# A state-space scan in one ring of buffers, its step sizes summed on TensorE, and a mixer without square root

## The reference

```python
def _ssm_layer(x, A_log, Dp, W_dbc, W_dt, b_dt):
    A = -jnp.exp(A_log)
    dbc = jnp.einsum('ble,ce->blc', x, W_dbc)
    delta, Bm, Cm = jnp.split(dbc, [DT_RANK, DT_RANK + N_STATE], axis=-1)
    delta = jax.nn.softplus(jnp.einsum('blr,er->ble', delta, W_dt) + b_dt)
    dA = jnp.exp(delta[..., None] * A)
    dBx = (delta * x)[..., None] * Bm[:, :, None, :]
    ...
    _, hs = jax.lax.associative_scan(combine, (dA, dBx), axis=1)   # h = dA * h + dBx
    y = jnp.einsum('blen,bln->ble', hs, Cm)
    return y + Dp * x
```

## Time and profile before

| | |
|---|---|
| median of 3 runs | 6798.75 us (6796.87 to 6824.71) |
| the profiled execution | 6804.28 us, its span 6802.5 us |
| busy: PE, DVE, ACT, POOL | 72%, 93%, 72%, 89% |
| stage one | to about 6192 us |
| stage two | from there to the end |
| DMA | 1561 MB, mean 229 GB/s |

### The profile page before, as it was taken

How to read it: one execution, slowest core, us unless ns; L and a number is a source line. 1 busy time by engine, 2 the same in 40 slices (tenths; PEclk the granted TensorE clock), 3 DMA queues, 4 the chain that set the end, 5 groups by cost and what they waited for, 6 DMA issues and landing times. The chain is left out here.

```text
span 6802.5 us, 114118 instructions
## 1 busy us (share of the span) xinstructions
PE 4903.7 (72%) x32336; PEld 1829.8 (27%) x32336; DVE 6322.3 (93%) x4435; ACT 4927.0 (72%) x10217; POOL 6080.2 (89%) x1940
## 2 busy tenths in 40 slices
PE   5777777777777777777777777677777777774777
PEld 1222222222222222222222222222222222222443
DVE  8999999999999999999999999999999999995554
ACT  6777777777777777777777777777777777772111
POOL 8999999999999999999999999999999999993110
PEclk8777777778777777778778787877777777776888
DMA  6777777777777777777777777777777777772000
GB/s 231 255 250 253 250 256 254 244 252 259 251 253 255 256 255 252 247 251 257 253 255 254 255 254 252 249 253 256 253 253 254 258 250 251 249 248 83 5 7 7
DMA packets 559826, 1561.16 MB, mean 229 GB/s; under 512 B 171938, under 2 KB 317858, under 8 KB 559586
## 3 DMA queue, kind: packets, MB, share of 16 engines
q1 hardware_dynamic: 559714, 1559.89, 68.9%
HBM read 1468.97 MB, written 90.59 MB: 229 GB/s over the span
## 5 line engine op out<-in xcount | busy, mean ns | idle before, releaser
L649 POOL TENSOR_TENSOR u<-dxb,Bt 128x1488 f32<-128x1488 f32 x1792 | 5909.1, 3342 | 134.0 <-DMA dxb<-dx_rows 129.3
L577 DVE TENSOR_TENSOR_SCAN hT<-decay,u 128x744 f32<-128x744 f32 x3584 | 5808.3, 1684 | 138.4 <-ACT decay L409 124.3
L409 ACT ACTIVATE decay<-decay,a_neg 128x371 f32<-128x371 f32 (+2 forms) x7168 | 3632.0, 556 | 652.7 <-PE decay L294 623.4
L294 PE MATMUL decay<-stk,spread 96*128 96x371 bf16 (+2 forms) x7168 | 2152.3, 394 | 1662.6 <-DVE hT L577 1628.2
L312 PE MATMUL z_bank<-hT,Cst 128*32 128x256 f32 x21504 | 1941.3, 493 | 7.6 <-ACT z_sb L418 4.1
L294 PEld LDWEIGHTS decay<-stk,spread 96*128 96x128 bf16 x7168 | 470.2, 104 | 3427.5 <-DVE hT L577 2821.7
L418 ACT COPY z_sb<-z_bank 128x512 f32<-128x512 f32 x1344 | 805.5, 599 | 643.2 <-PE z_bank L312 628.8
L312 PEld LDWEIGHTS z_bank<-hT,Cst 128*32 128x32 f32 x21504 | 664.6, 130 | 972.1 <-issue 770.0
L1092 POOL TENSOR_TENSOR wr<-pr 128x744 f32<-128x744 f32 x8 | 14.1, 1760 | 437.4 <-DVE pr L1015 437.4
L910 ACT ACTIVATE relu<-PB,c_b 128x744 f32<-128x744 f32 x64 | 56.4, 881 | 232.6 <-PE PB L788 232.6
L352 PE MATMUL prep_bank<-tmap,yT 64*128 64x32 f32 (+3 forms) x1344 | 212.6, 295 | 0.0
(11 more groups left out here) (151 smaller groups left out, 2217.0 us busy)
## 6 DMA issues: line engine op xcount, KB each, us to landing
dxb<-dx_rows SPq DMA_DIRECT2D x3584, 372.0 KB, 4.4
delta_parts<-parts SPq DMA_DIRECT2D x112, 279.0 KB, 5.8
stk<-delta_parts SPq DMA_DIRECT2D x112, 279.0 KB, 3.1
y_rows<-z_sb SPq DMA_DIRECT2D x1792, 12.0 KB
yT<-y_rows SPq DMA_DIRECT2D x112, 192.0 KB, 3.3
dx_rows<-dx SPq DMA_DIRECT2D x112, 186.0 KB, 2.3
xT<-in_x SPq DMA_DIRECT2D x64, 186.0 KB, 4.8
xP<-in_x SPq DMA_DIRECT2D x64, 186.0 KB, 4.5
```

The lines of the kernel that those rows point to most:

```text
L294: nc.tensor.matmul(slot[:, e, :, 1:], spread[0:PARTS * QR, TILES_G * q + er // TILES_G, :], src[:, er % TILES_G, :, 1:], start=True, stop= ...
L409: last = nc.scalar.activation(bank, bank, ACT.Exp, scale=a_neg[:, l, c:c + 1])
L577: nc.vector.tensor_tensor_scan(hT[q % 2][:, i * PAIR:(i + 1) * PAIR], pair_slot(p), u[c % U_RING][:, part * PAIR:(part + 1) * PAIR], 0.0, ...
L649: tt(u[c % U_RING][:, :].rearrange(channels, t=W0), dxb[slot][:, :].rearrange(channels, t=W0), Bt[buf][:, :].unsqueeze(1).broadcast_to([P, ...
```

## The change

One ring. The buffers dxb are gone. There are four buffers u of 2976 columns, eight channels each (`HALVES` = 2 chunks). The broadcast loads dx straight into a half of u, and GpSimd multiplies it by Bt in place, one instruction of 2976 columns a product, 8 a group. A broadcast now waits for the scans that read its half before, not for a product. VectorE waits for u once in four pairs.

```diff
+                prod, half = divmod(c, HALVES)
-                if not known_below(n, 1) or c >= BC_RING:
-                    sp.wait_ge(s_u, BC_RING * (turn - 1) + slot + 1)
+                if not known_below(n, 1) or prod >= RING:
+                    sp.wait_ge(s_scan, PAIRS * n + CHUNK * (c + 1 - HALVES * RING))
...
-                    sp.dma_start(dxb[slot][b:P:2, :], src).then_inc(s_bc[slot], 16)
+                    dst = u[prod % RING][b:P:2, half * CHUNK * PAIR:(half + 1) * CHUNK * PAIR]
+                    sp.dma_start(dst, src).then_inc(s_bc[prod % RING], 16)
...
-                tt(u[c % U_RING][:, :].rearrange(channels, t=W0), dxb[slot][:, :].rearrange(channels, t=W0),
-                   Bt[buf][:, :].unsqueeze(1).broadcast_to([P, 2 * CHUNK, W0]), ALU.mult).then_inc(s_u, 1)
+                here = u[slot][:, :].rearrange("p (e t) -> p e t", t=W0)
+                tt(here, here, Bt[buf][:, :].unsqueeze(1).broadcast_to([P, 2 * HALVES * CHUNK, W0]), ALU.mult).then_inc(s_u, 1)
```

```diff
-                    if c == 0 and after:
+                    if c == 0:
+                        store_parts(here)
+                    if c == 1 and before:
+                        load_yT(before)
+                    if c == 3:
+                        load_stack(here, half)
+                    if c == 4 and after:
                         load_x(after, 1 - half)
-                    if c == 3 and before:
+                    if c == 7 and before:
                         store_h(before)
-                    if c == 4 and prev:
+                    if c == 8 and prev:
                         reload_x(prev)
-                    if 5 <= c < 13 and prev:
-                        for t in range(2 * (c - 5), 2 * (c - 4)):
+                    if c >= 10 and prev:
+                        for t in range(3 * (c - 10), min(3 * (c - 9), TB)):
                             diagonal(prev, 1 - half, t)
-                    if c == 13 and after:
+                    if c == 15 and after:
                         store_dx(after, 1 - half)
```

```diff
+            def sum_delta(at, i):
...
+                if i == 0:
+                    pe.wait_ge(s_w, n + 1)
+                    pe.wait_ge(s_read, 3 * n + 1)
+                    nc.tensor.matmul(bank, eye[:, :], t_w[:, :], start=True, stop=False)
+                elif i == 1:
+                    pe.wait_ge(s_one, n + 1)
+                    nc.tensor.matmul(bank, eye[:, :], t_one[:, :], start=False, stop=False)
+                    nc.tensor.matmul(bank, ones[0:1, 0:P], ones[0:1, P:], start=False, stop=False)
+                else:
+                    pe.wait_ge(s_ln, n + 1)
+                    nc.tensor.matmul(bank, eye[:, :], t_ln[:, :], start=False, stop=False)
+                    pe.wait_ge(s_relu, n + 1)
+                    nc.tensor.matmul(bank, eye[:, :], t_relu[:, :], start=False, stop=True).then_inc(s_delta, 1)
+
+            def take_off(at, i):
...
+                if i == 0:
+                    pe.wait_ge(s_hi, n + 1)
+                    pe.wait_ge(s_dx, n + 1)
+                else:
+                    pe.wait_ge(s_mid, n + 1)
+                nc.tensor.matmul(prep[:, 0:W0], eye[:, :], delta[:, :], start=True, stop=False)
+                for j in range(i + 1):
+                    last = nc.tensor.matmul(prep[:, 0:W0], neg_eye[:, :], parts[:, j, :], start=False, stop=(j == i))
+                last.then_inc((s_rest, s_rest2)[i], 1)
...
+                    if after and p in (5, 7, 8):
+                        sum_delta(after, (5, 7, 8).index(p))
+                    if after and p in (13, 16):
+                        take_off(after, (13, 16).index(p))
```

dx on VectorE, from the bank prep behind pair 9, and no longer on GpSimd:

```diff
+                dve.wait_ge(s_hi, n + 1)
+                dve.wait_ge(s_x, 16 * (n + 1))
...
+                tt(dx[:, :], prep[:, 0:W0], xT[buf][:, :], ALU.mult).then_inc(s_dx, 1)
```

```diff
-                nc.scalar.activation(flat(dst), banks(src), ACT.Sqrt, bias=eps[:, 0:1]).then_inc(s["std"], 1)
+                nc.scalar.activation(flat(log), banks(src), ACT.Ln, bias=eps[:, 0:1]).then_inc(s["log"], 1)
+                act.wait_ge(s["log"], c + 1)
+                nc.scalar.activation(dst[:, :], log[:, :], ACT.Exp, scale=-0.5).then_inc(s["rstd"], 1)
...
-                dve.wait_ge(s["std"], c + 1)
-                nc.vector.reciprocal(rs[:, :], st[:, :]).then_inc(s["rstd"], 1)
```

More of the change, by code:

```diff
@@ L84, in ssm_stage @@
         stk = [sb(f"stk{i}", [P, TILES_G, W0], BF16) for i in range(2)]
-        dxb = [sb(f"dxb{i}", [P, CHUNK * PAIR]) for i in range(BC_RING)]
-        u = [sb(f"u{i}", [P, CHUNK * PAIR]) for i in range(U_RING)]
+        u = [sb(f"u{i}", [P, HALVES * CHUNK * PAIR]) for i in range(RING)]
         hT = [sb(f"hT{i}", [P, (EPT + 1) * W0]) for i in range(2)]
@@ L91, in ssm_stage @@
         t_v, t_abs, t_w = [sb(n, [P, W0]) for n in ("t_v", "t_abs", "t_w")]
-        t_one, t_sum, delta, dx = [sb(n, [P, W0]) for n in ("t_one", "t_sum", "delta", "dx")]
+        t_one, t_ln, t_relu, delta, dx = [sb(n, [P, W0]) for n in ("t_one", "t_ln", "t_relu", "delta", "dx")]
+        eye, neg_eye = sb("eye", [P, P]), sb("neg_eye", [P, P], BF16)
+        ones = sb("ones", [1, P + W0], BF16)
         db = [ps(f"decay{i}", 2 * BANK) for i in range(SLOTS)]
@@ L259, in _ @@
             store_dx(first, 0)
-            store_parts(first)
-            load_stack(first, 0)
             layer_bodies(sp, body)
+            load_yT(BEFORE_LAST)
             store_h(BEFORE_LAST)
@@ L367, in body @@
                         item(after, 1 - half, (1, 19, 23).index(p))
+                    if after and p in (5, 7, 8):
+                        sum_delta(after, (5, 7, 8).index(p))
+                    if after and p in (13, 16):
+                        take_off(after, (13, 16).index(p))
                     if prev and p in (27, 29):
                         to_channels(prev, after, (27, 29).index(p))
+            first = (0, 0)
+            item(first, 0, 0)
             for i in range(3):
-                item((0, 0), 0, i)
+                sum_delta(first, i)
+            take_off(first, 0)
+            take_off(first, 1)
+            item(first, 0, 1)
+            item(first, 0, 2)
             layer_bodies(pe, body)
@@ L455, in decayed @@
                 act.wait_ge(s_abs, G(at) + 1)
+                if not known_below(G(at), 1):
+                    act.wait_ge(s_delta, G(at))
                 nc.scalar.activation(t_w[:, :], t_abs[:, :], ACT.Exp, scale=-1.0).then_inc(s_w, 1)
@@ L541, in _ @@
             high(first)
-            lay_high(first)
             middle(first)
-            lay_middle(first)
+            low(first)
             take_B(first, 0)
@@ L613, in body @@
                     scan(here, p)
-                    if not after:
-                        continue
-                    if p == 6:
-                        rest_of_one(after)
-                    if p == 8:
-                        log1p(after)
-                    if p == 10:
-                        add_relu(after)
-                    if p == 13:
-                        rest(after)
-                    if p == 16:
-                        low(after)
-            first = (0, 0)
-            rest_of_one(first)
-            log1p(first)
-            add_relu(first)
-            rest(first)
-            low(first)
+                    if after and p == 9:
+                        times_x(after, 1 - half)
+            times_x((0, 0), 0)
             layer_bodies(dve, body)
@@ L889, in _ @@
             act.wait_ge(s_set, 2)
+            nc.scalar.add_instruction(mybir.InstLoadActFuncSet(
+                name=nc.get_next_instruction_name(), engine=mybir.EngineType.Activation, ins=[], outs=[],
+                act_func_set_id=EXPS_ON_JOINT_TABLE))
             def square(s, c, xc, sq):
@@ L912, in _ @@
             square(sA, 0, xcA, sqA)
-            std(sA, 0, PA0, stA)
+            inverse_std(sA, 0, PA0, stA, rsA)
             with act.Fori(1, chunks) as i:
@@ L1066, in _ @@
             center(sA, 0, PA0, xcA)
-            scale(sA, 0, stA, rsA, xcA, uA)
+            scale(sA, 0, rsA, xcA, uA)
             a3(0), a3b(0), a4(0)
```

161 lines of the change are left out of this document (58 added, 103 removed).

## The result

The change makes the kernel slower: 7022.99 us (7008.68 to 7052.51) beside 6804.18 for the kernel before on the same chip, a ratio of **1.032 [1.028, 1.036]**. The forecast was 6580, in a range of 6450 to 6730. The first lines of the page of the kernel after (they answer to the earlier trace rows) show that no engine became the bound: all are less busy in a longer span, VectorE 87% instead of 93.

The account below looks back on a forecast made before the run. VectorE was taken as the bound, at 54.74 us a group. From 6798.75, terms of -197 (VectorE), +22 (ScalarE), +6 (start) and -50 (mixer) sum to -219, giving 6580 us, range 6450 to 6730.

Parts of the forecast that it names:

- VectorE (1): Scans: five small VectorE operations a group become one, each displacing 0.44 us; -197 us, floor 51.6 us a group.
- hold of a shared port: VectorE beside GpSimd: a two-SBUF-input operation could wait a whole product, 6.4 us; none seen, so the sum was left unchanged.
- GpSimd (2): Eight products of 2976 columns a group at 6.38 us, 51.0 in all, bound 6.60 each; off the path, 0.
- R2: Rival: GpSimd takes over as bound, product at 6.60 plus 1.2 us DMA wait, 54.0 a group; 6672 us, chance 0.13.
- The ring's cover (3): Ring and SyncE queue: 7.3 us of cover for products, 2.6 for the yT load with a 4.4 us landing; cost 0.
- The clock at the new work (4): TensorE: new products fall into empty pairs, clock expected high there, low behind 24/25 and 31/0; old stalls left at 1.3 us.
- R1: Rival: TensorE stays at its low clock under the added work and scans stop; 6915 us, chance 0.08.
- Start (6): Kernel start: the first product needs both halves and takes 6.4 instead of 3.3 us; +6 us, bounds +3 and +12.
- ScalarE (5): ScalarE in the scan groups: two operations behind pairs 1, 3, 5 and 9; +0.2 us a group, +22 us.
- Mixer (7): Mixer after the scans: Exp on ScalarE replaces the reciprocals, 5.0 us less plus 1.5 from the clock; -50 us.
- R3: Rival: stalls return elsewhere (yT late behind pair 27, middle part at 16), 1.3 us a group; 6704 us, chance 0.12.
- R4: Rival: the high clock removes the old stalls too, 51.9 us a group; 6437 us, chance 0.12.

Follow-up runs that it names:

- e7: Changed kernel with yT loaded early, idle products behind pairs 24, 25, 31 and 0, and 64 already fulfilled waits ahead of ScalarE's first group: 6533.70 us, ratio 0.960.
- e12: Changed kernel with yT loaded early, plus 64 already fulfilled waits ahead of ScalarE's first group, without idle products: 6707.82 us, ratio 0.984.
- e1: Changed kernel with one edit, the load of yT issued behind the last diagonal (broadcast 15) instead of behind broadcast 1: 6756.19 us, ratio 0.991.
- e5: e1 plus three idle bf16 products of 512 columns on TensorE behind pairs 24 and 25: 6592.28 us, ratio 0.968.
- e6: e1 plus three idle bf16 products of 512 columns on TensorE behind pairs 24, 25, 31 and 0: 6555.01 us, ratio 0.963.
- the control: e6 with its idle products cut from 512 to 8 columns, same instructions and waits: 6758.43 us, ratio 0.991.
- e3: Changed kernel with the load of yT behind broadcast 0, two scans earlier and ahead of the store of the parts: 6760.98 us, ratio 0.991.

## Why the prediction was wrong

Right were these steps. **VectorE (1):** 18 scans take 28.86 us, 1.60 each, and dx displaces 0.44 (3001.03 to 3001.47). No hold of a shared port shows beside products of 6.5 us. **GpSimd (2):** four products take 25.83 us, 6.46 each, where 6.38 was forecast and 6.60 was the bound, and the scans never wait for one; in e7 GpSimd still idles 157.6 us. R2 did not come. **The ring's cover (3):** in the changed kernel the scans wait for ScalarE's decay (568.9 of 572.3 us) and not for the ring. **The clock at the new work (4):** high, as shown above, and no gap of note behind pairs 3 to 26; R1 did not come. **Start (6):** +7.1 for +6. **ScalarE (5):** the +0.2 stands about where it was put, behind pairs 1 to 3, by the layers compared below. **Mixer (7):** -60 behind the last scan for -50; from rsA to pr it was 11.37 us and is now 6667.24 - 6662.59 = 4.65, 6.7 less for the 5.0 + 1.5:

```profile
6662.59 0.82 ACT L890 ACTIVATE rsA<-stA 128x744 f32<-128x744 f32 x1
...
6663.44 0.93 DVE L1001 TENSOR_TENSOR uA<-xcA,rsA 128x744 f32<-128x744 f32 x1 [2.97 <-ACT rsA L890]
6664.43 1.52 PE L776 MATMUL PA<-uA,c_b_re 128*128 128x372 f32 x4 [1.53 <-DVE uA L1001]
...
6667.24 0.93 DVE L1006 TENSOR_TENSOR pr<-PA,T1R 128x744 f32<-128x744 f32 x1 [1.24 <-PE PA L776]
```

The error is 7023 - 6580 = 443 us, and the runs divide it into three parts.

**Step (3), "a landing that I take as long as the broadcast's, 4.4 ... so 2.6 us of cover": 267 us.** The step saw the right place, the right wait and the right consequence, and sized the landing by a row of another transfer. It is 8.0 us, so from the broadcast's issue at 3018.24 it takes 10.1 us instead of 6.2, and TensorE wanted it after 8.3 (the 8.8 of the forecast, less what the wait for dx had made the queue late, a wait that the step did not have). The page of before had a landing of yT, 3.3, which would have misled further: it was for a load with nothing large ahead of it. The row that bore on it was the store of the parts, 279 KB and 5.8 us to land, which the change puts between two broadcasts just ahead of yT in the same queue, with a DMA share near 1 in that stretch (0.97 between 3018 and 3023). The cover was good for a landing of 4.4 + 2.6 = 7.0; an estimate from these two rows, 5.8 + 3.3 = 9.1, is over it. The cost was then put at 0 with no chance of its own. R3 named this stall, at 1.3 us a group in all; it cost 2.4, and with the clock held up 2.9.

**Step (4), "the old stalls ... I leave them at 1.3 us": 128 us.** The clock was foretold, low behind 24/25 and 31/0; the price was not. In e12 the gaps behind pairs 27 to 31 and 1 to 3 sum to 2.64 us, where the forecast had 1.3 of old stalls and 0.2 from step (5); 1.14 x 112 = 128. As 0.44 of the 2.64 is the seam of layer 0 just shown, layers without instruction loads tell it more cleanly (us a group):

```
                     behind 27 to 30   behind 1 to 3   period
layer 0, before            0.58             0.64        54.68
layer 0, e1                1.75             0.77        54.20
layer 1, before            0.42             0.71        54.59
layer 1, e12               1.98             0.87        54.49
```

Against the 53.2 of the forecast that is 1.0 and 1.3 us a group too much. Behind pairs 1 to 3 there are 0.13 to 0.16 more than before, near step (5)'s 0.2. The growth is behind pairs 27 to 30, and e5, e6 and the control show that it hangs on the clock. Why the same low clock costs three to nearly five times as much there is not settled. The clock comes back later: at the start of pair 27's scan it is low in 60 to 70% of the groups of e1 and e12, before in 40%.

**Code loading, in no step: 48 us** (e1 less e12, as far as e12 took it away). The kernel before has such a stall too, but only in layer 2: 1.8 us behind pair 31 of every second group.

267 + 48 + 128 make up the 443, but only because they are differences of medians. The runs were made on different chips, on which the kernel before differs by 14 us (6804 to 6819); by the ratios the parts are 278, 52 and 113. The mixer's 10 us more than forecast are in the last part.

R4, that the high clock removes the old stalls as well, was the one rival pointing to what can be had: 51.9 us a group; e7 comes to 52.75 by keeping the clock up on purpose.

## What to carry to other kernels

Moving a load within a queue changes its landing as well as its start: size it by what stands ahead of it in the new place, as a cautious bound the landings of both in a row (it held here: 8.0 us against 9.1), and give a tight cover a price and a chance instead of 0. Where an engine with a gated clock has short bursts between long waits, look for the stretches in which it has least to do, not for its mean: a few idle products there gave 3% here, more than the change does even without its late load (0.9%, all of it the mixer's), and a saving on the bound engine can vanish whole into the waits of another one. And when a change moves the code of a loop, compare its layers or iterations one by one; a stall in every second one, with the engine waiting for nothing, is no matter of the change's logic, and can move to another layer rather than go.

## What the runs showed of the hardware

- The same load of 192 KB lands in 3.3 us behind one small store and the store of dx (e1), in 5.4 behind one broadcast (e3) and in 8.0 behind two broadcasts and a store of 279 KB (after).
- Three products of 512 columns behind each of four pairs that hold only decays took the granted clock from 0.862 to 0.947 over the span and the time from 6756 to 6555; with 8 columns, nothing (0.855 to 0.865 and 6758).
- A loop's code is loaded again on every turn in some layers, in pieces of 8 KB (1.05 MB in 128 loads of after; in e1 five loads for two groups in layer 1, none in layer 0). At the seam of the loop ScalarE was held for 2.6 us (e1) and 2.2 (e12) in the rows shown; the scans of e1 waited 4.5 there. 64 instructions ahead of the loop moved the loads and the stall from layer 1 to layer 0. The Trainium skill (Runtime: NRT & Kernel Launch, "Instruction fetch mechanics") says that a branch taken to a page of code that is not at hand costs a fetch before the engine goes on. That fits stalls at the seam of a loop; the size it gives for a block, 16 KiB, is not what these loads show.
- A GpSimd product of 2976 columns written over its own input takes 6.46 us, 2.17 ns a column, no more than two products of 1488 columns into another tile (2 x 3.30).
